# Moving the SBUF addresses of the operands of an expert layer so that each stationary block starts 64 bytes after its moving rows, modulo 512

## The chip, the cores and the metric

The kernel runs on one core of one Trainium2 chip. The metric is the time of one execution in microseconds of device time. The numbers given as "before" come from three executions that were only timed, and from one further execution that the hardware profiler recorded; that one is the source of all rows below.

## The reference

The input x holds 32 sequences of 512 tokens with 256 channels, in float32. What is computed, cut to what matters here:

```python
x  = L0_attn_x                              # 32 x 512 x 256
xn = layernorm(x)
x  = x + attention(xn, Wq, Wk, Wv, Wo, ...) + experts(xn, gate_w, w1, w2)

# attention: 16 heads of 16 channels, no softmax: scores are multiplied by a decay mask
scores = einsum('bhid,bhjd->bhij', q, k) * mask
out    = einsum('bhij,bhjd->bhid', scores, v)   # then Wo and a group norm

# experts: 8 of them; each takes the 128 tokens of a sequence with the highest probability
probs        = softmax(einsum('BTC,CE->BTE', x, gate_w), axis=-1)
top_p, top_i = top_k(probs.transpose(0, 2, 1), 128)
xin = take(x, top_i)                            # 32 x 8 x 128 x 256
h   = gelu(einsum('BElC,ECH->BElH', xin, w1))   # w1: 8 x 256 x 1024
y   = einsum('BElH,EHC->BElC', h, w2)           # w2: 8 x 1024 x 256
out = zeros.at[top_i].add(y * top_p)
```

## The kernel before

The work is written by hand, one instruction stream for each engine, with semaphores between them; no scheduler decides an order. There are two parts, one after the other.

**Attention** runs over the 32 sequences b, in a software pipeline: while sequence b has its scores and values computed, b+1 has its queries, keys and values projected and b-1 its output projection. Products in which accuracy matters are split: every float32 operand is held as a high part (`x_hi`, `w_hi`) and a low part (`x_lo`, `w_lo`) of type float32r, and a product is the sum of three matmuls, high by high, high by low, low by high. The projections of queries, keys and outputs (`query_key`, `project`, through `product`, L1383) have the weights as stationary operand and 512 token columns as moving operand. The projection of values and gate scores (`value_gate`, L1449, L1451, L1453) has 128 tokens as stationary operand and 272 or 256 weight columns as moving operand.

**The experts** follow in 64 steps. A step n is one expert e and a group of four sequences (512 chosen tokens, `SL`; one half of them is `HALF`, 256). The order is `ORDER`: experts 0 and 1 alternate in blocks of four groups, then experts 2 to 7 come one after the other with eight steps each. In a step, TensorE does:

- eight transposes of the gathered rows (`transposes`, L1688), which are moving 128 columns of an identity;
- the first expert matrix as seven products of quadrants (a Strassen-Winograd scheme, `product1` to `product7`, all through `quarter`, L1698): seven products, two halves A and B of each, two column blocks, three terms, which is 84 matmuls. Stationary is a block of 128 columns of `w1h` or `w1l`, moving are the 256 columns of one slot of `xs_hi` or `xs_lo`;
- the second expert matrix (`down`, L1779): four token blocks, eight pieces of the hidden dimension, three terms, which is 96 matmuls. Stationary is a block of 128 tokens of `g_hi` or `g_lo` (the hidden values after the gelu, split), moving are the 256 columns of one piece of `w2h` or `w2l`.

That is 188 matmuls a step, each with a weight load of its own. The weights of an expert are split on ScalarE (high parts) and GpSimd (low parts) while the expert before runs; they have two sets of buffers, index `e % 2`, so that even experts read one set of addresses and odd experts the other. `xs_hi`, `xs_lo`, `g_hi` and `g_lo` have one set.

The expert part has no memory of its own: nearly all its tiles lie over tiles of the attention part, at addresses that are written out as numbers (`at(name, shape, dtype, offset)`), while the attention's tiles get theirs one behind the other (`sb`). A column block of a stationary operand and a slot, piece or token row of a moving operand begin a multiple of 512 bytes after their tile, so the tile's start modulo 512 holds for all of them. The starts modulo 512 before, and the distance d = (stationary start minus moving start) modulo 512 that follows:

```
product                     stationary      moving          d
w1, even experts            w1h, w1l   0    xs_hi/lo 160    352 (high and low weights)
w1, odd experts, high       w1h      128    xs_hi/lo 160    480
w1, odd experts, low        w1l      160    xs_hi    160    0
w2, even experts            g_hi/lo  160    w2h, w2l 128    32
w2, odd experts, w2h        g_hi/lo  160    w2h      160    0
w2, odd experts, w2l        g_hi     160    w2l 160 or 64   0 or 96 (pieces 0-3 or 4-7)
attention, L1383            w, 448          x, a      96    352
attention, L1449-L1453      x, 96           vg, w    448/0  160 or 96
```

The instruction stream interleaves the weight load for the next matmul with the matmul that is running, so the moving rows of one matmul and the stationary block of the next are read at the same time. Inside a step the next block stands at the same distance as the own one, with few exceptions at the seams between products.

Of the kernel before, what the change touches and what calls it, by code (L numbers as in the profile page):

```python
# [42 lines left out]
NSUB = S // SUB  # L43
# [4 lines left out]
GRP = 4  # L48
# [192 lines left out]
def layer(nc, x, xn_d, out, wq, wk, wv, wo, gw, w1, w2, bvr, cst_d, vec_d):  # L241
    with ExitStack() as ctx:
        def sb(name, shape, dt=F32):
            return ctx.enter_context(nc.sbuf_tensor(name, shape, dt))

        def at(name, shape, dt, offset):

            return nc.alloc_sbuf_tensor_at(name, shape, dt, offset=offset)

        def sem(name):  # L250
            return ctx.enter_context(nc.semaphore(name))

# [13 lines left out]
        w_lo = [sb(f"w_lo{i}", [P, DH, D], F32R) for i in range(4)]
        vg_hi = sb("vg_hi", [P, DH, VG], F32R)
        xb = [sb(f"x{i}", [P, TT, D]) for i in range(2)]
        xn = sb("xn", [P, TT, D])
        vraw = sb("v_unbiased", [P, TT, VG])  # L270
        st = sb("ln_stats", [P, TT, 6])
        mv = sb("ln_mv", [P, TT, 2])
        ln_ve, ln_r, ln_y, ln_a, ln_m = (sb(f"ln_{n}", [P, TT]) for n in ("ve", "r", "y", "a", "m"))
        x_hi = sb("x_hi", [P, DH, S], F32R)
        x_lo = sb("x_lo", [P, DH, S], F32R)
        q32 = sb("q32", [P, DH, S])
        qm = [sb(f"q_parity{i}", [P, DH, 2, S]) for i in range(2)]
        qd = [sb(f"q_decayed{i}", [P, DH, S]) for i in range(2)]
        k32 = [sb(f"k{i}", [P, DH, S]) for i in range(2)]
        kn = sb("k_natural", [P, TT, D])  # L280
        vm = [sb(f"v_parity{i}", [P, TT, VW]) for i in range(2)]
        tm = [sb(f"state{i}", [P, NSUB - 1, DH, 2 * HD]) for i in range(2)]
        s_sb = [sb(f"s_sb{i}", [P, PAIRS, 512]) for i in range(2)]
        a_hi = sb("a_hi", [P, DH, S], F32R)
        a_lo = sb("a_lo", [P, DH, S], F32R)
        o32 = sb("o32", [P, DH, S])
        ost = sb("o_stats", [P, DH, 6])
        gm = sb("g_moments", [P, DH, 2])
        gs = sb("g_means", [P, DH, 2])
        gn_ve, gn_r, gn_y, gn_a, gn_m, gn_s, gn_b = (sb(f"gn_{n}", [P, DH])  # L290
                                                     for n in ("ve", "r", "y", "a", "m", "s", "b"))
# [19 lines left out]
        ln_mv = sem("ln_mv_ready")  # L311
# [65 lines left out]
        def has(b):  # L377
# [2 lines left out]

        SL = GRP * CAP
        HALF = SL // 2
        K1 = 7 * QF * 4
        K2 = FT * D * 4
        KX = 7 * HALF * 4
        LATE = 186880
        w1h = [at("w1_hi0", [P, 7, QF], F32R, LATE), at("w1_hi1", [P, 7, QF], F32R, 56448)]
        w1l = [at("w1_lo0", [P, 7, QF], F32R, LATE + K1), at("w1_lo1", [P, 7, QF], F32R, 167584)]
        s2 = at("w2_stage", [P, FT, D], F32, LATE + 2 * K1)
# [3 lines left out]
        xg = [at(f"xg{k}", [P, D], F32, 53248 + 1024 * k if k < 3 else LATE + 2 * K1 + K2) for k in range(GRP)]  # L393
        idx = at("step_idx", [P, GRP], U32, LATE + 2 * K1 + K2 + 1024)
        sidx = at("scatter_idx", [P, GRP], U32, LATE + 2 * K1 + K2 + 1056)
        xs_hi = at("xs_hi", [P, 7, HALF], F32R, 87712)
        xs_lo = at("xs_lo", [P, 7, HALF], F32R, 87712 + KX)
        xsum = at("x_sums", [P, 4, HALF], F32, 87712 + 2 * KX)
        hid = {q: at(f"hidden{q}", [P, 2, 2, HALF], F32, o)
               for q, o in (("22", 114336), ("21", 118432), ("11", 122528), ("12", 130720))}  # L400
        y = [at("y", [P, GRP, D], F32, 126624), res]
# [1509 lines left out]
```

## Time and profile before

| what | value |
|---|---|
| median of three timed runs | 2347.25 us (2346.27 to 2350.14) |
| profiled execution, its time | 2340.57 us |
| profiled execution, its span (first to last instruction) | 2338.6 us |
| matmuls, and weight loads | 34252 each |
| TensorE (PE) busy | 2264.5 us, 97% of the span |
| VectorE, ScalarE, GpSimd busy | 1531.5, 1391.5, 1283.3 us (65, 59, 55%) |

The profile lists what each engine did and when. PE is TensorE's matmuls and PEld its weight loads, which run beside them. Matmuls are pipelined: a row of one matmul is longer than the time until the next one starts, so the pace of a stream of matmuls is read from the distance between starts, or from the length of a window and the count in it, not from a row's duration. The span ends with the expert part, which begins at about 895 us.

### The profile page before, as it was taken

How to read it: one execution, taken by the hardware profiler on the slowest of the kernel's cores; microseconds unless marked ns; L12 is line 12 of the kernel's file. 1: busy time of each engine (PE TensorE's matmuls, PEld its weight loads, DVE VectorE, ACT ScalarE, POOL GpSimd, SP SyncE). 2: the span in 40 equal slices, each digit the busy share in tenths (PEclk: the TensorE clock that was granted, in tenths of full speed). 3: DMA queues.
4: the chain of work that ended last, by engine and by line, in shares of the span. 5: the costliest groups of instructions: out<-in, count | busy, mean ns of one | idle time of the engine just before them, and what ended most of it. 6: DMA issues, size and time to landing. Idle time of an engine off the chain costs nothing.

```text
span 2338.6 us, 81411 instructions
## 1 busy us (share of the span) xinstructions
PE 2264.5 (97%) x34252; PEld 2095.6 (90%) x34252; DVE 1531.5 (65%) x3103; ACT 1391.5 (59%) x2553; POOL 1283.3 (55%) x2012
## 2 busy tenths in 40 slices
PE   6999999999999988999999999999999999999998
PEld 5777777777777778999999999999999999999998
DVE  3555555656666657996766767667667667676674
ACT  4555565555655546556666656666666666666664
POOL 4444444444544455655566666666566576575453
PEclk9999999999999999999999999999999999999999
DMA  3232222322223312232324324224234233232332
GB/s 120 74 95 85 75 76 83 94 84 76 76 75 94 98 61 71 49 77 50 50 44 89 46 46 91 43 49 86 47 52 82 47 54 80 48 54 43 51 50 33
DMA packets 129368, 157.72 MB, mean 67 GB/s; under 512 B 11008, under 2 KB 118656, under 8 KB 129024
## 3 DMA queue, kind: packets, MB, share of 16 engines
q0 software_dynamic: 49152, 67.14, 17.8%
q1 hardware_dynamic: 79872, 85.54, 11.6%
q8 instruction: 272, 4.46, 0.8%
q14 instruction: 72, 0.59, 0.1%
HBM read 85.53 MB, written 67.11 MB: 65 GB/s over the span
## 4 chain that ended last, share of the span: by engine, by line
PE 55%; DVE 0%; POOL 0%; issue 0%; ACT 0%; DVEq 0%
PE attn L1779 28%; PE scores L1698 18%; PE front L1698 7%; PE front L1688 2%; POOL out L798 0%; DVE rows L211 0%; DVE topi L207 0%; DVE top L202 0%; DVE hidden L1263 0%; DVE xs_lo L1233 0%; ACT res L949 0%; DVE rows L223 0%; PE scores L233 0%; PE scores L232 0%; DVE rows L225 0%
## 5 line engine op out<-in xcount | busy, mean ns | idle before, releaser
L1779 PE MATMUL attn<-w_hi,g_hi 128*128 128x256 f32 x2048 | 581.5, 284 | 2.5 <-DVE g_lo L1274 2.4
L1779 PE MATMUL attn<-w_lo,g_hi 128*128 128x256 f32 x2048 | 578.3, 282 | 0.0
L1779 PE MATMUL attn<-w_hi,g_lo 128*128 128x256 f32 x2048 | 578.1, 282 | 0.0
L987 ACT ACTIVATE hidden<-hidden 128x512 f32<-128x512 f32 x384 | 235.4, 629 | 263.9 <-DVE hidden L1263 263.9
L1779 PEld LDWEIGHTS attn<-w_hi,g_hi 128*128 128x128 f32 x2048 | 388.6, 190 | 3.0 <-DVE g_lo L1274 2.7
L1779 PEld LDWEIGHTS attn<-w_hi,g_lo 128*128 128x128 f32 x2048 | 388.3, 190 | 0.0
L1779 PEld LDWEIGHTS attn<-w_lo,g_hi 128*128 128x128 f32 x2048 | 388.0, 189 | 0.0
L1698 PE MATMUL scores<-xs_hi,w_hi 128*128 128x256 f32 x1280 | 362.0, 283 | 8.4 <-DVE xs_lo L1233 6.3
L1698 PE MATMUL scores<-xs_lo,w_hi 128*128 128x256 f32 x1280 | 362.8, 283 | 0.0
L1263 DVE TENSOR_TENSOR hidden<-front,hidden 128x512 f32<-128x512 f32 x256 | 176.3, 689 | 284.0 <-PE front L1698 270.7
L1698 PE MATMUL scores<-xs_hi,w_lo 128*128 128x256 f32 x1280 | 361.0, 282 | 0.0
L1274 DVE TENSOR_TENSOR g_lo<-hidden,g_hi 128x512 fp32r<-128x512 f32 x512 | 348.3, 695 | 9.9 <-ACT g_hi L991 7.6
L718 POOL DMA_INDIRECT out<-y,scatter_idx x128 | 220.3, 1721 | 235.6 <-ACT y L949 206.1
L708 POOL DMA_INDIRECT xg<-xn_rows,step_idx x256 | 278.0, 1086 | 101.3 <-issue 64.2
L718 POOL DMA_INDIRECT out<-res,scatter_idx x124 | 212.6, 1714 | 203.6 <-ACT res L949 167.5
L1698 PEld LDWEIGHTS scores<-xs_hi,w_hi 128*128 128x128 f32 x1280 | 243.3, 190 | 9.9 <-issue 9.2
L1698 PEld LDWEIGHTS scores<-xs_lo,w_hi 128*128 128x128 f32 x1280 | 243.0, 190 | 0.0
L1698 PEld LDWEIGHTS scores<-xs_hi,w_lo 128*128 128x128 f32 x1280 | 242.8, 190 | 0.0
L1263 DVE TENSOR_TENSOR hidden<-scores,hidden 128x512 f32<-128x512 f32 x256 | 172.5, 691 | 78.3 <-PE scores L1698 77.0
L1123 DVE TENSOR_TENSOR s_sb<-scores,cst 128x1024 f32<-128x1024 f32 x128 | 149.8, 1212 | 83.4 <-PE scores L1490 83.4
L610 POOL TENSOR_TENSOR v_parity<-v_unbiased,bv_rows 128x256 f32<-128x256 f32 x128 | 92.2, 730 | 152.2 <-ACT v_unbiased L848 149.7
L991 ACT ACTIVATE g_hi<-hidden 128x512 fp32r<-128x512 f32 x256 | 161.8, 632 | 6.1
(182 smaller groups left out, 5154.4 us busy)
## 6 DMA issues: line engine op xcount, KB each, us to landing
x<-in_x SPq DMA_DIRECT2D x32, 512.0 KB, 5.3
w_stage<-in_w SPq DMA_DIRECT2D x16, 1024.0 KB, 6.4
xn_rows<-xn SPq DMA_DIRECT2D x32, 512.0 KB, 3.2
res<-in_x SPq DMA_DIRECT2D x32, 512.0 KB, 3.8
out<-res SPq DMA_DIRECT2D x32, 512.0 KB, 3.4
xg<-xn_rows,step_idx POOLq DMA_INDIRECT x256
out<-y,scatter_idx POOLq DMA_INDIRECT x128, 3.9
out<-res,scatter_idx POOLq DMA_INDIRECT x128, 3.9
```

Source lines behind the costliest of these rows:

```text
L610: pool.tensor_tensor(own, spread(vraw[:, t, 0:D]), spread(bv[:]), ALU.add).then_inc(vm_ready, 1)
L708: pool.indirect_dma_start(xg[k][:], None, xn_d, bass.IndirectOffsetOnAxis(idx[:, k:k + 1], 0)).then_inc(gathered, 16)
L718: pool.indirect_dma_start(out_rows, bass.IndirectOffsetOnAxis(sidx[:, k:k + 1], 0), y[g % 2][:, k, :], None, compute_op=ALU.add).then_inc( ...
L987: act.activation(own(q, p), src, ACT.Gelu).then_inc(g_ready, 1)
L991: act.activation(quadrant(g_hi, q, p), own(q, p), ACT.Copy).then_inc(gh_act, 1)
L1123: dve.tensor_tensor(s_sb[z][:, banks, :].rearrange("p k (g i) -> p (k g) i", i=SUB), sbk[:, banks, :].rearrange("p k (g i) -> p (k g) i", ...
L1263: dve.tensor_tensor(dst, a, b, ALU.add).then_inc(sum_ready, 1)
L1274: dve.tensor_tensor(quadrant(g_lo, q, p), own(q, p), quadrant(g_hi, q, p).bitcast(F32), ALU.subtract).then_inc(gl_ready, 1)
L1688: last = pe.transpose(tb[:, h, k * P:(k + 1) * P], xg[k][:, h * P:(h + 1) * P], ident)
L1698: last = pe.matmul(dst, w_[par][:, w, cols], x__[:, x_, :], start=first and m == 0 and i == 0, stop=i == 2, skip_group_check=True)
L1779: last = pe.matmul(yb[k % 2][:, 0:D], g_[:, m, cols], w, start=start and m == first and i == 0, stop=end, skip_group_check=True)
```

## The change

Only SBUF addresses change. Every instruction of every engine is the same in number, order, shape and semaphores as before; the order of the program shows no other difference than the names of buffers. Small tiles move to the front of the memory, the attention's large tiles get written-out addresses at multiples of 512 (`tm[1]` and the first column block of `vraw` aside), and the expert part's tiles are laid out anew over them. The starts modulo 512 after:

```
product                     stationary      moving          d
w1, all experts             w1h, w1l   0    xs_hi/lo 448    64
w2, all experts             g_hi/lo   64    w2h, w2l   0    64
attention, L1383            w          0    x, a       0    0
attention, L1449-L1453      x          0    vg, w   0/64    0 or 448
```

The core of the diff:

```diff
-        w_hi = [None if i == 2 else sb(f"w_hi{i}", [P, DH, D], F32R) for i in range(4)]
-        x_hi = sb("x_hi", [P, DH, S], F32R)
-        x_lo = sb("x_lo", [P, DH, S], F32R)
...
+        KB = 1024
+        w_hi = [None if i == 2 else at(f"w_hi{i}", [P, DH, D], F32R, o * KB)
+                for i, o in enumerate((54, 56, None, 58))]
...
+        x_hi = at("x_hi", [P, DH, S], F32R, 143 * KB)
+        x_lo = at("x_lo", [P, DH, S], F32R, 147 * KB)
...
-        LATE = 186880
-        w1h = [at("w1_hi0", [P, 7, QF], F32R, LATE), at("w1_hi1", [P, 7, QF], F32R, 56448)]
-        w1l = [at("w1_lo0", [P, 7, QF], F32R, LATE + K1), at("w1_lo1", [P, 7, QF], F32R, 167584)]
-        w2h = [at("w2_hi0", [P, FT, D], F32R, 78976), at("w2_hi1", [P, FT, D], F32R, 106144)]
-               for i, os in enumerate(((70784, 74880), (181920, LATE + 2 * K1 + K2 + 1088)))]
-        xs_hi = at("xs_hi", [P, 7, HALF], F32R, 87712)
-        xs_lo = at("xs_lo", [P, 7, HALF], F32R, 87712 + KX)
-        g_hi = at("g_hi", [P, FT, SL], F32R, 134816)
-        g_lo = at("g_lo", [P, FT, SL], F32R, 151200)
...
+        G_AT = 87 * KB + 64
+        X_AT = 143 * KB + 448
+        w1h = [at("w1_hi0", [P, 7, QF], F32R, 183 * KB + 512), at("w1_hi1", [P, 7, QF], F32R, 57 * KB)]
+        w1l = [at("w1_lo0", [P, 7, QF], F32R, 197 * KB + 512), at("w1_lo1", [P, 7, QF], F32R, 169 * KB + 512)]
+        w2h = [at("w2_hi0", [P, FT, D], F32R, 79 * KB), at("w2_hi1", [P, FT, D], F32R, 157 * KB + 512)]
+               for i, os in enumerate(((71 * KB, 75 * KB), (165 * KB + 512, 219 * KB + 512)))]
+        g_hi = at("g_hi", [P, FT, SL], F32R, G_AT)
+        g_lo = at("g_lo", [P, FT, SL], F32R, G_AT + FT * SL * 4)
+        xs_hi = at("xs_hi", [P, 7, HALF], F32R, X_AT)
+        xs_lo = at("xs_lo", [P, 7, HALF], F32R, X_AT + 7 * HALF * 4)
```

## Rows read from the trace of the kernel before

**Rows 1.** The page's part 1 (busy us, share, count) and TensorE's granted clock.

```profile
PE 2264.5 (97%) x34252; PEld 2095.6 (90%) x34252; DVE 1531.5 (65%) x3103; ACT 1391.5 (59%) x2553; POOL 1283.3 (55%) x2012
...
PEclk9999999999999999999999999999999999999999
```

**Rows 2.** Windows: experts 2 to 5, eight steps each (length, busy us and count, clock).

```profile
1271.44:1448.63 177.19, 177.19 (x1506) 177.19 (x1505) 122.27 (x225) 112.78 (x208) 113.56 (x100) 1.00 0.33 60
1448.63:1626.96 178.33, 178.33 (x1506) 178.33 (x1505) 122.43 (x225) 112.76 (x208) 114.06 (x100) 1.00 0.33 60
1626.96:1804.16 177.19, 177.19 (x1506) 177.19 (x1505) 122.27 (x225) 112.79 (x208) 113.53 (x100) 1.00 0.33 61
1804.16:1982.49 178.33, 178.33 (x1506) 178.33 (x1505) 122.75 (x225) 112.89 (x208) 113.76 (x100) 1.00 0.33 60
```

**Rows 3.** Groups by form: TensorE's matmuls (count, busy us, mean ns, idle before).

```profile
L1779 PE MATMUL attn<-w_hi,g_hi 128*128 128x256 f32 x2048 | 581.5, 284 | 2.5 <-DVE g_lo L1274 2.4
...
L1698 PE MATMUL scores<-xs_hi,w_hi 128*128 128x256 f32 x1280 | 362.0, 283 | 8.4 <-DVE xs_lo L1233 6.3 <-DVE res L1170 1.7 <-DVE hidden L1263 0.5
...
L1698 PE MATMUL front<-xs_hi,w_hi 128*128 128x256 f32 x512 | 144.2, 282 | 0.0
...
L1383 PE MATMUL front<-x_hi,w_hi 128*128 128x512 f32 x256 | 109.0, 426 | 4.0 <-DVE x_lo L1136 4.0
...
L1449 PE MATMUL front<-vg_hi,x_hi 128*128 128x272 f32 x256 | 86.9, 339 | 0.0
...
L1383 PE MATMUL front<-a_hi,w_hi 128*128 128x512 f32 x124 | 49.7, 401 | 0.0
```

**Rows 4.** Timeline of TensorE, expert 4: transposes (start us, duration us, instruction).

```profile
1651.23 1.04 PE L1688 MATMUL front<-cst,xg 128*128 128x128 f32 x8
1652.03 0.37 PE L1779 MATMUL attn<-w_hi,g_hi 128*128 128x256 f32 x1
1652.23 0.28 PE L1779 MATMUL attn<-w_lo,g_hi 128*128 128x256 f32 x1
```

**Rows 5.** Timeline, expert 4, w2 pieces: first and last of 24 matmuls, d = 32.

```profile
1654.24 0.28 PE L1779 MATMUL attn<-w_hi,g_hi 128*128 128x256 f32 x1
...
1656.96 0.28 PE L1779 MATMUL attn<-w_hi,g_lo 128*128 128x256 f32 x1
```

**Rows 6.** Timeline, expert 5, w2 pieces 0-3: first and last of 24, d = 0.

```profile
1831.60 0.28 PE L1779 MATMUL attn<-w_hi,g_hi 128*128 128x256 f32 x1
...
1834.36 0.28 PE L1779 MATMUL attn<-w_hi,g_lo 128*128 128x256 f32 x1
```

**Rows 7.** Timeline, expert 4, w1 products: first and last of 36 matmuls, d = 352.

```profile
1666.99 0.28 PE L1698 MATMUL scores<-xs_hi,w_hi 128*128 128x256 f32 x1
...
1671.15 0.28 PE L1698 MATMUL front<-xs_hi,w_lo 128*128 128x256 f32 x1
```

**Rows 8.** Timeline, expert 1, one w1 product: two neighbouring column blocks, d = 0.

```profile
1201.89 0.28 PE L1698 MATMUL front<-xs_lo,w_hi 128*128 128x256 f32 x1
1202.00 0.28 PE L1698 MATMUL front<-xs_hi,w_lo 128*128 128x256 f32 x1
...
1202.24 0.29 PE L1698 MATMUL front<-xs_lo,w_hi 128*128 128x256 f32 x1
1202.37 0.28 PE L1698 MATMUL front<-xs_hi,w_lo 128*128 128x256 f32 x1
```

**Rows 9.** Timeline, attention, 512 moving columns: first and last of six matmuls, d = 352.

```profile
599.78 0.40 PE L1383 MATMUL front<-a_hi,w_hi 128*128 128x512 f32 x1
...
600.95 0.39 PE L1383 MATMUL front<-a_hi,w_lo 128*128 128x512 f32 x1
```

**Rows 10.** Timeline of weight loads beside Rows 9: two neighbours.

```profile
600.25 0.19 PEld L1383 LDWEIGHTS front<-a_hi,w_hi 128*128 128x128 f32 x1
600.49 0.19 PEld L1383 LDWEIGHTS front<-a_lo,w_hi 128*128 128x128 f32 x1
```

**Rows 11.** Window: attention, 300 to 800 us (columns as in Rows 2).

```profile
300.00:800.00 500.00, 483.99 (x12925) 386.50 (x12924) 306.42 (x737) 284.25 (x527) 233.56 (x729) 1.00 0.28 85
```

**Rows 12.** The page's part 4: the chain that ended last.

```profile
PE attn L1779 28%; PE scores L1698 18%; PE front L1698 7%; PE front L1688 2%; POOL out L798 0%; DVE rows L211 0%; DVE topi L207 0%; DVE top L202 0%; DVE hidden L1263 0%; DVE xs_lo L1233 0%; ACT res L949 0%; DVE rows L223 0%; PE scores L233 0%; PE scores L232 0%; DVE rows L225 0%
```

More of the change, by code:

```diff
@@ L254, in layer @@
         vec = sb("vec", [P, V_N])
+        gst_w = sb("gate_stage", [P, DH, E])
+        st = sb("ln_stats", [P, TT, 6])
+        mv = sb("ln_mv", [P, TT, 2])
+        ln_ve, ln_r, ln_y, ln_a, ln_m = (sb(f"ln_{n}", [P, TT]) for n in ("ve", "r", "y", "a", "m"))
+        ost = sb("o_stats", [P, DH, 6])
+        gm = sb("g_moments", [P, DH, 2])
+        gs = sb("g_means", [P, DH, 2])
+        gn_ve, gn_r, gn_y, gn_a, gn_m, gn_s, gn_b = (sb(f"gn_{n}", [P, DH])
+                                                     for n in ("ve", "r", "y", "a", "m", "s", "b"))
+        idx = sb("step_idx", [P, GRP], U32)
+        sidx = sb("scatter_idx", [P, GRP], U32)
         route = Routing(ctx, nc, cst)
@@ L261, in layer @@
         wst = s1[:, 0:4, :].rearrange("p a (b n) -> p (a b) n", n=D).rearrange("p (i h) n -> p i h n", h=DH)
-        gst_w = sb("gate_stage", [P, DH, E])
-        bv = sb("bv_rows", [P, D])
-        w_hi = [None if i == 2 else sb(f"w_hi{i}", [P, DH, D], F32R) for i in range(4)]
[L266 to L270, printed above, removed]
@@ L271, in layer @@
-        st = sb("ln_stats", [P, TT, 6])
-        mv = sb("ln_mv", [P, TT, 2])
-        ln_ve, ln_r, ln_y, ln_a, ln_m = (sb(f"ln_{n}", [P, TT]) for n in ("ve", "r", "y", "a", "m"))
-        x_hi = sb("x_hi", [P, DH, S], F32R)
-        x_lo = sb("x_lo", [P, DH, S], F32R)
[L276 to L289, printed above, removed]
@@ L290, in layer @@
-        gn_ve, gn_r, gn_y, gn_a, gn_m, gn_s, gn_b = (sb(f"gn_{n}", [P, DH])
-                                                     for n in ("ve", "r", "y", "a", "m", "s", "b"))
+        KB = 1024
+        bv = at("bv_rows", [P, D], F32, 53 * KB)
+        w_hi = [None if i == 2 else at(f"w_hi{i}", [P, DH, D], F32R, o * KB)
+                for i, o in enumerate((54, 56, None, 58))]
+        w_lo = [at(f"w_lo{i}", [P, DH, D], F32R, (60 + 2 * i) * KB) for i in range(4)]
+        xb = [at(f"x{i}", [P, TT, D], F32, (68 + 4 * i) * KB) for i in range(2)]
@@ new lines, in layer @@
+        xn = at("xn", [P, TT, D], F32, 76 * KB)
+        vg_hi = at("vg_hi", [P, DH, VG], F32R, 80 * KB)
+        vraw = at("v_unbiased", [P, TT, VG], F32, 80 * KB + DH * VG * 4)
+        tm = [at(f"state{i}", [P, NSUB - 1, DH, 2 * HD], F32, 90 * KB - (2 - i) * (NSUB - 1) * DH * 2 * HD * 4)
+              for i in range(2)]
+        kn = at("k_natural", [P, TT, D], F32, 90 * KB)
+        k32 = [at(f"k{i}", [P, DH, S], F32, o * KB) for i, o in enumerate((127, 94))]
+        qd = [at(f"q_decayed{i}", [P, DH, S], F32, o * KB) for i, o in enumerate((131, 98))]
@@ new lines, in layer @@
+        qm = [at(f"q_parity{i}", [P, DH, 2, S], F32, o * KB) for i, o in enumerate((135, 102))]
+        vm = [at(f"v_parity{i}", [P, TT, VW], F32, 110 * KB + i * TT * VW * 4) for i in range(2)]
+        x_hi = at("x_hi", [P, DH, S], F32R, 143 * KB)
+        x_lo = at("x_lo", [P, DH, S], F32R, 147 * KB)
+        q32 = at("q32", [P, DH, S], F32, 151 * KB)
+        s_sb = [at(f"s_sb{i}", [P, PAIRS, 512], F32, (155 + 8 * i) * KB) for i in range(2)]
+        a_hi = at("a_hi", [P, DH, S], F32R, 171 * KB)
@@ L293, in layer @@
+        a_lo = at("a_lo", [P, DH, S], F32R, 175 * KB)
+        o32 = at("o32", [P, DH, S], F32, 179 * KB)
         tb = ctx.enter_context(nc.psum_tensor("front", [P, DH, 512], F32))
@@ new lines, in layer @@
+        w2h = [at("w2_hi0", [P, FT, D], F32R, 79 * KB), at("w2_hi1", [P, FT, D], F32R, 157 * KB + 512)]
+        w2l = [[at(f"w2_lo{i}{j}", [P, FT // 2, D], F32R, o) for j, o in enumerate(os)]
+               for i, os in enumerate(((71 * KB, 75 * KB), (165 * KB + 512, 219 * KB + 512)))]
+        xg = [at(f"xg{k}", [P, D], F32, (53 + k) * KB) for k in range(GRP)]
+        g_hi = at("g_hi", [P, FT, SL], F32R, G_AT)
+        g_lo = at("g_lo", [P, FT, SL], F32R, G_AT + FT * SL * 4)
+        hid = {q: at(f"hidden{q}", [P, 2, 2, HALF], F32, G_AT + o * KB)
+               for q, o in (("22", 32), ("21", 36), ("11", 44), ("12", 48))}
```

14 lines of the change are left out of this document (3 added, 11 removed).

## The prediction

> **What bounds the kernel now.** I read the page first. TensorE's matmuls are busy for 97% of the span, no other engine for more than 65% [rows 1]. The granted clock stands at its upper level (2.4 GHz) in all 40 slices, so the clock has nothing to give. The chain that ended last is TensorE almost alone: `down` 28%, the w1 products 25%, the transposes 2%; every entry of another engine rounds to nothing [rows 12].
>
> Next come windows cut at the borders of single experts [rows 2]. In each of them TensorE's busy time is the window's whole length, while VectorE has 122 of 177 us, ScalarE and GpSimd 113. So from there to the end no wait is on the path, and a nanosecond more or less for each matmul goes into the time undiminished. The windows also show how regular this is: the two even experts take 177.19 us, the two odd ones 178.33, to the last digit, with the same instructions. All that differs is the buffer set, that is, the addresses. Eight steps of 188 matmuls make 1504 (two more records reach over the edges), so a step is 22.149 us in an even expert and 22.291 in an odd one. The eight transposes and the first matmul after them take 1652.23 − 1651.23 = 1.00 us [rows 4]; the other 179 matmuls take (22.149 − 1.00) / 179 = 118.15 ns each in even experts and 118.94 in odd ones. The counts of the whole program, three terms of each row, are 3 × 2048 in `down` and 3 × (1280 + 512) in the w1 products [rows 3], 11520 in all, 180 for each of the 64 steps.
>
> One column per clock would be 256 / 2.4 = 106.7 ns. So each of these matmuls takes about 11.8 ns longer than its columns alone. That is the sum the change could draw on; the question is how much of it comes from two reads of SBUF that meet, the running matmul's moving rows and the next one's stationary block.
>
> **What the trace says on the distance d.** The timeline gives paces at three distances. 24 matmuls at d = 32 take (1656.96 − 1654.24) / 23 = 118.3 ns each [rows 5], 24 at d = 0 take 120.0 [rows 6], 36 at d = 352 take 118.9 [rows 7]. Addresses matter more at single places: in one w1 product of an odd expert, where d = 0 for the low weights, the matmul with `xs_lo` takes 0.11 us in one column block and 0.13 in the next [rows 8]; 512 bytes are all that separates the two blocks. The distance 64 occurs nowhere.
>
> How much can the meeting of the reads cost at all? In attention six matmuls with 512 moving columns and d = 352 start 234.0 ns apart [rows 9]. A weight load begins with each and its record is 0.19 us long [rows 10]; the eight loads of the transposes pass in 0.80 us [rows 4], so a load reads for at most about 100 ns. The second half of a 512-column matmul thus has no load beside it. With 118.9 ns for the first half (the same d, a load beside it) the second takes 234.0 − 118.9 = 115.1. So most of the extra 11.8 ns is there without any load, and a load at d = 352 adds about 3.8.
>
> **The change part by part.** It removes and adds no instruction, DMA or wait; nothing moves in a queue. The terms are three.
>
> First, all 11456 matmuls of the expert part that count here (179 × 64) go to d = 64. From below their pace is bounded by the matmul without a load, 115.1 ns; from above by the slowest long stretch, 120.0. The nearest rows are those at d = 32. I take 117.2, about a third of the way from 118.3 down to the floor: one distance everywhere does away with the dear places (d = 0, in most of the odd experts' matmuls), and a block that keeps a fixed lead over the rows should meet them less often, but rows 32 bytes beside it show no deep dip, so I do not take more. Even experts then gain 118.15 − 117.2 = 0.95 ns, odd ones 118.94 − 117.2 = 1.74; half of the steps each, 1.345 × 11456 = 15.4 us less. At the floor it would be 3.445 × 11456 = 39.5 us less, at 120.0 it would be 1.455 × 11456 = 16.7 us more.
>
> Second, attention's split products leave d = 352 (and 160 or 96) for d = 0 (or 448). They are 3 × (256 + 124) with 512 columns and 3 × 256 in `value_gate` [rows 3], 1908. At worst each pays the difference between d = 0 and d = 32, 120.0 − 118.3 = 1.7 ns, 3.2 us; at best nothing. TensorE is busy for 484 of 500 us there [rows 11], so nearly all of it would reach the path; I take 3 us.
>
> Third, the other engines' tiles move too. Where they work slower, 55 us in 177 on VectorE hide it in the expert part [rows 2]; I take nothing. If that cover were gone, TensorE would wait at L1698 for `xs_lo`, where it idles for 6.3 us now [rows 3].
>
> The sum is −15.4 + 3 = −12.4 us. The profiled execution took 2340.57 us, 6.7 below the median of the timed ones; I apply the difference to the median: 2347.25 − 12.4 = 2335.
>
> **A rule against it.** The product with two paces [rows 8] and the 177.19 against 178.33 us [rows 2] say that TensorE's reads do get in each other's way, by 1 to 10 ns. The Trainium skill says otherwise: "TensorE: Matmul & The Clock Gate" (Part 2, step 1) gives the weight load and the moving operand an independent SBUF read port each, and "SBUF — State Buffer" (Who interferes with whom) states "PE and ACT never wait on anyone". By that rule the sum would be zero and the time 2347; the trace does not agree with it.
>
> **The rivals.** *Distance does nothing* (0.25). The reads' cost may hang on higher address bits or on the phase that the stream happens to be in; 512 bytes turned 0.11 into 0.13 us without a change of d [rows 8], which speaks for it. Then 64 is like 32: a pace of 118.3 in both kinds of expert changes +0.15 and −0.64 ns, on the mean −0.245 × 11456 = −2.8 us, and attention's 3 us give it back: 2347, between 2342 and 2352.
>
> *Blocks on equal phase are the slow ones* (0.23), the rival on the other side. d = 0 and d = 64 share that block and rows start at the same place within 64 bytes; d = 32, 96, 352 and 480 do not. The 120.0 of [rows 6] would then be the price of that equality, and all expert matmuls would pay it: +16.7 + 3.2 = +19.9 us, 2367. Against it: half the blocks of [rows 8] take 0.11 us at d = 0. It decides once the common pace is above the present mean of 118.55; with attention's loss, from 118.3 on the kernel is no faster.
>
> *The whole extra time goes* (0.06). If the moving rows wait only because of how loads lie, the pace falls to 106.7 ns: 11.85 × 11456 = 136 us, 2211. The second halves at 115.1 without a load speak against it [rows 9, 10].
>
> **How the numbers follow.** The forecast case, a pace between 115.1 and 118, has 0.46; its own range is 2308 to 2342. A measurement of this kernel can tell 0.2%, some 4.7 us, from no change. Faster are the forecast case, the last rival and a few hundredths at the edge of the first: 0.54. The rest of the first makes "same" 0.23 after a little of it goes either way; slower has 0.23. The range from 2308 (the floor, attention unchanged) to 2360 leaves out the last rival and the dear end of the second, under 2 in 10.
>
> **What would show it.** In the windows of single experts, even and odd ones should have one length, near 8 × (1.00 + 179 × 0.1172) = 175.8 us. If they stay at 177 to 178 the first rival holds; at 179.8 (120.0 ns) the second; at 160.8 the third. The two column blocks of [rows 8] should take the same time. The 512-column matmuls of [rows 9] should stand at 234 to 236 ns. I am wrong if a distance that the trace has never shown behaves unlike its neighbours, which is where my 117.2 is chosen and not read; or if VectorE's or ScalarE's groups get longer and TensorE shows idle time in the expert windows.

## The result, and the profile after

The changed kernel takes 2316.52 us (median of four runs, 2313.94 to 2321.24); the kernel before takes 2346.76 beside it (four runs, 2346.1 to 2350.14). The ratio is 0.9871, with a 95% interval from 0.9852 to 0.9889: faster by 30.2 us, where 12.4 were forecast. The profiled execution is the slowest of the four, 2321.24 us, with a span of 2319.3.

On the page of the kernel after, TensorE's busy time (part 1) and its granted clock (part 2) answer to [rows 1]. TensorE is busy for 29.6 us less, in the same number of matmuls:

```profile
PE 2234.9 (96%) x34252; PEld 2068.1 (89%) x34252; DVE 1522.3 (66%) x3103; ACT 1390.6 (60%) x2553; POOL 1271.4 (55%) x2012
...
PEclk9999999999999998999999999999999999999999
```

Windows of experts 2 to 5 of the kernel after, with the columns of [rows 2] (behind the clock stand the busy share of the DMA engines and GB/s):

```profile
1271.90:1446.33 174.43, 174.43 (x1506) 174.43 (x1505) 121.48 (x225) 112.61 (x208) 112.00 (x100) 1.00 0.34 60
1446.33:1620.75 174.43, 174.43 (x1506) 174.43 (x1505) 121.46 (x225) 112.51 (x208) 112.60 (x100) 1.00 0.34 61
1620.75:1795.18 174.43, 174.43 (x1506) 174.43 (x1505) 121.50 (x225) 112.60 (x208) 111.98 (x100) 1.00 0.34 62
1795.18:1969.61 174.43, 174.43 (x1506) 174.43 (x1505) 121.47 (x225) 112.57 (x208) 112.36 (x100) 1.00 0.34 62
```

Even and odd experts now have one length, TensorE still fills the whole window, and the other engines are as busy as before. An even expert is 2.76 us shorter and an odd one 3.90 [rows 2]; carried over to all eight experts, four of each make 11.0 + 15.6 = 26.6 us, nearly all of the gain. A step is 174.43 / 8 = 21.80 us and the mean pace (21.80 − 1.00) / 179 = 116.2 ns.

That mean hides two paces. The timeline of TensorE in expert 4 of the kernel after shows first and last of 24 `down` matmuls, then the first, the fourth and the last of 36 w1 matmuls:

```profile
1713.05 0.28 PE L1779 MATMUL attn<-w_hi,g_hi 128*128 128x256 f32 x1
...
1715.75 0.28 PE L1779 MATMUL attn<-w_hi,g_lo 128*128 128x256 f32 x1
...
1725.66 0.29 PE L1698 MATMUL scores<-xs_hi,w_hi 128*128 128x256 f32 x1
...
1726.02 0.28 PE L1698 MATMUL scores<-xs_hi,w_hi 128*128 128x256 f32 x1
...
1729.65 0.28 PE L1698 MATMUL front<-xs_hi,w_lo 128*128 128x256 f32 x1
```

`down` runs at (1715.75 − 1713.05) / 23 = 117.4 ns to the digits shown (117.7 with the trace's nanoseconds), as forecast. The w1 stretch starts with 0.12 us a matmul and from the fourth on takes (1729.65 − 1726.02) / 32 = 113.4 ns, 113.33 by the nanoseconds: 272 clocks at 2.4 GHz for 256 columns, the same from matmul to matmul. That is below the 115.1 that the prediction took for a floor. Both stand at d = 64. The alternation of [rows 8] is gone.

In attention, six matmuls with 512 columns answer to [rows 9], d now 0 (timeline, kernel after):

```profile
601.92 0.39 PE L1383 MATMUL front<-a_hi,w_hi 128*128 128x512 f32 x1
...
603.05 0.39 PE L1383 MATMUL front<-a_hi,w_lo 128*128 128x512 f32 x1
```

They start (603.05 − 601.92) / 5 = 226 ns apart instead of 234.0; over all output projections of the trace the mean is 226.7 (544 clocks). The query and key projections, twice as many, come down less: they start 229.8 ns apart on the mean, 233.9 before, because each run of them opens with about five starts of 228 to 236 ns before it settles at 226.7.

One thing the profiled execution lost has another cause. Its first `down` begins at 911.1 us, 12.5 later than before (898.6). Up to the last but one group norm of attention (848.1 us, 846.8 before) the lag is 1.3 us; the rest arises at the passage from attention to the experts. A window of it, first before and then after:

```profile
855.00:905.00 50.00, 39.53 (x824) 35.17 (x824) 32.44 (x75) 25.66 (x45) 23.46 (x48) 0.90 0.29 87
865.00:915.00 50.00, 36.05 (x663) 31.72 (x653) 31.60 (x68) 17.27 (x28) 13.51 (x33) 0.75 0.24 76
```

The granted clock there is 0.75 on the mean, 0.90 before: for half of the 50 us it is at the lower of its two levels (1.2 and 2.4 GHz), where before it was for a fifth. TensorE is busy for 36 of them. Two runs of one and the same program, below as e2 and e11, reach the first `down` at 912.5 and 897.3 us. So some 15 us between single executions need not come from addresses, and below I read causes from windows and paces and take a single time only as a rough check.

### The profile page after: what moved, and what is told of

Read it like the earlier page. It is cut to its first block, busy times and chain, and to the rows that moved or that the text cites. A ratio compares the mean times of both kernels' runs of the same rounds, so it can differ in the third digit from the quotient of the medians.

```text
span 2319.3 us, 81411 instructions
## 1 busy us (share of the span) xinstructions
PE 2234.9 (96%) x34252; PEld 2068.1 (89%) x34252; DVE 1522.3 (66%) x3103; ACT 1390.6 (60%) x2553; POOL 1271.4 (55%) x2012
## 3 DMA queue, kind: packets, MB, share of 16 engines
q1 hardware_dynamic: 79872, 85.54, 11.5%
## 4 chain that ended last, share of the span: by engine, by line
PE 54%; DVE 0%; POOL 0%; issue 0%; ACT 0%; DVEq 0%
PE attn L1779 28%; PE scores L1698 17%; PE front L1698 7%; PE front L1688 2%; POOL out L798 0%; DVE rows L211 0%; DVE topi L207 0%; DVE top L202 0%; DVE hidden L1263 0%; DVE xs_lo L1233 0%; ACT res L949 0%; DVE rows L223 0%; PE scores L233 0%; PE scores L232 0%; DVE rows L225 0%
## 5 line engine op out<-in xcount | busy, mean ns | idle before, releaser
L1698 PE MATMUL scores<-xs_lo,w_hi 128*128 128x256 f32 x1280 | 356.4, 278 | 0.0
L1698 PE MATMUL scores<-xs_hi,w_lo 128*128 128x256 f32 x1280 | 356.0, 278 | 0.0
L1274 DVE TENSOR_TENSOR g_lo<-hidden,g_hi 128x512 fp32r<-128x512 f32 x512 | 340.7, 685 | 9.5 <-ACT g_hi L991 7.0
L718 POOL DMA_INDIRECT out<-y,scatter_idx x128 | 214.7, 1677 | 222.1 <-ACT y L949 192.6
```

The lines of the kernel that those rows point to most:

```text
L718: pool.indirect_dma_start(out_rows, bass.IndirectOffsetOnAxis(sidx[:, k:k + 1], 0), y[g % 2][:, k, :], None, compute_op=ALU.add).then_inc( ...
L1274: dve.tensor_tensor(quadrant(g_lo, q, p), own(q, p), quadrant(g_hi, q, p).bitcast(F32), ALU.subtract).then_inc(gl_ready, 1)
L1698: last = pe.matmul(dst, w_[par][:, w, cols], x__[:, x_, :], start=first and m == 0 and i == 0, stop=i == 2, skip_group_check=True)
```

## The experiments

All of them change addresses only, against the kernel after; the expected texts were written in three batches (e1 to e4, e5 to e8, e9 to e12), each on one chip with runs of the kernel before, and each names its theories anew. A pair below is (stationary start, moving start) modulo 512. A seam is the place where one product follows another; its distance is that of the new product's first block to the rows of the old product's last matmul. "Step" is the mean of eight steps, even experts / odd experts; before it is 22.15 / 22.29 us, after 21.80 / 21.80.

| run | w1 pair, even / odd | w2 pair, even / odd | step | time, us | before, same chip |
|---|---|---|---|---|---|
| e1 | 0,448 / 0,448 | 0,0 / 0,448 | 21.93 / 21.29 | 2312.68 | 2347.40 |
| e2 | 0,160 / 0,160 | 32,0 / 32,0 | 22.17 / 22.17 | 2346.07 | 2347.40 |
| e3 | 0,0 / 0,0 | 0,0 / 0,256 | 22.46 / 22.46 | 2354.47 | 2347.40 |
| e4 | 0,448 / 0,448 | 64,0 / 64,0 | 21.80 / 21.80 | 2327.01 | 2347.40 |
| e5 | 0,448 / 0,448 | 0,448 / 0,448 | 21.29 / 21.29 | 2281.48 | 2341.94 |
| e6 | 32,480 / 0,480 | 128,0 / 128,0 | 22.09 / 22.16 | 2334.42 | 2341.94 |
| e7 | 0,384 / 0,384 | 256,0 / 256,0 | 22.30 / 22.30 | 2341.76 | 2341.94 |
| e8 | 64,0 / 0,0 | 448,0 / 448,0 | 21.63 / 22.17 | 2312.41 | 2341.94 |
| e9 | 64,0 / 0,0 | 64,0 / 64,0 | 21.78 / 22.07 | 2319.69 | 2341.13 |
| e10 | 64,0 / 0,0 | 0,448 / 0,0 | 21.94 / 22.33 | 2331.24 | 2341.13 |
| e11 | as e2 | as e2 | 22.17 / 22.17 | 2335.95 | 2341.13 |
| e12 | 0,64 / 0,64 | 0,0 / 0,64 | 22.31 / 22.08 | 2336.80 | 2341.13 |

(In odd experts of e6, e8, e9 and e10 the low weights of w2's pieces 4 to 7, a sixth of `down`, start at 32, 64, 64 and 448 instead. Times are single ones, but for the medians of e5, five runs, and e11, seven; of before there are one, nine and ten runs in the three batches.)

**e1: hidden values at 0, second matrix of odd experts at 448.**

```diff
-        G_AT = 87 * KB + 64
+        G_AT = 87 * KB
-        ... at("w2_hi1", [P, FT, D], F32R, 157 * KB + 512)
+        ... at("w2_hi1", [P, FT, D], F32R, 157 * KB + 448)
-        ... (165 * KB + 512, 219 * KB + 512)
+        ... (165 * KB + 448, 219 * KB + 960)
```

> g_hi and g_lo start at 0 modulo 512 instead of 64; in odd experts w2 moves to 448, in even experts it stays at 0. So w2 has d = 0 in even experts and d = 64 in odd ones; w1 stays at d = 64 (stationary 0, moving 448). In the changed kernel the 24 w2 matmuls of pieces 0-3 go at 117.7 ns in both kinds of expert, the 36 w1 matmuls at 113.9. Theory 1 (the distance modulo 512 sets the pace): w2 of odd experts stays at 117.7, w2 of even experts goes up towards 120, so a step takes 21.80 us in odd and about 22.0 us in even experts. Theory 2 (the stationary block's own start decides, a multiple of 512 is fast): w2 goes to about 113.5 in both, a step takes about 21.4 us in both. Theory 3 (the moving rows' start decides, a multiple of 64 is fast): no change, 117.7 and 21.80 us in both.

Windows of expert 4 and expert 5, columns as above:

```profile
1618.05:1793.49 175.44, 175.44 (x1506) 175.44 (x1505) 121.57 (x225) 113.22 (x208) 112.06 (x100) 1.00 0.34 62
1793.49:1963.81 170.32, 170.32 (x1506) 170.32 (x1505) 122.45 (x225) 112.38 (x208) 113.82 (x100) 1.00 0.34 62
```

Even experts, with `down` at d = 0, have it at 120.00 ns (24 matmuls from 1710.88 to 1713.64 us). Odd ones, with `down` at d = 64, at 113.35 (1883.62 to 1886.23), with the w1 products at 113.34 too. The direction is that of the distance, but the same d = 64 in `down` is 117.7 in the kernel after and 113.35 here: d is not all.

**e2: back to distances that the kernel before had (w2 d = 32, w1 d = 352), at new places.**

```diff
-        G_AT = 87 * KB + 64
-        X_AT = 143 * KB + 448
+        G_AT = 87 * KB + 32
+        X_AT = 143 * KB + 160
```

> g at 32 and xs at 160 modulo 512: the distances of the even experts of the kernel before, d = 32 for w2 and d = 352 for w1, now in all experts, everything else as in the changed kernel. Theory 1 (distance modulo 512): the paces of before come back, w2 about 118.3, w1 about 118.9, a step of 22.15 us. Theory 2 (stationary start): w1 stays at 113.9 since its stationary blocks stay at 0, w2 about 118. Theory 3 (moving start): w1 goes to about 118, since its rows now start 32 bytes beside a multiple of 64, w2 stays at 117.7. Rival 4 (higher address bits, that is, the new places as such): both stay near 113.9 and 117.7.

```profile
1633.92:1811.30 177.38, 177.38 (x1506) 177.38 (x1505) 122.28 (x225) 112.84 (x208) 113.64 (x100) 1.00 0.33 61
1811.30:1988.69 177.39, 177.39 (x1506) 177.39 (x1505) 122.28 (x225) 112.84 (x208) 114.11 (x100) 1.00 0.34 61
```

In the windows of experts 4 and 5 the length of the even experts before [rows 2] is back, to 0.2 us, and for odd experts as well. The paces are 118.4 in `down` and 118.7 in w1, those of [rows 5, 7] within 0.2 ns. The layout itself is therefore worth nothing in the expert part: the start modulo 512 is what counts, not higher address bits and not which tile lies where.

**e3: everything at distance 0 or 256.**

```diff
-        G_AT = 87 * KB + 64
-        X_AT = 143 * KB + 448
+        G_AT = 87 * KB
+        X_AT = 143 * KB
-        ... "w2_hi1", ... 157 * KB + 512    ... (165 * KB + 512, 219 * KB + 512)
+        ... "w2_hi1", ... 157 * KB + 256    ... (165 * KB + 256, 219 * KB + 768)
```

> g and xs at 0 modulo 512, so w1 has d = 0 with both operands at 0; w2 has d = 0 in even experts, and in odd experts its rows are at 256, so d = 256. Theory 1 (distance): d = 0 is slow, w1 and the w2 of even experts at about 119 to 120. Theory 2 (stationary start): everything at about 113.5, a step of 21.3 to 21.4 us in both kinds of expert. Theory 3 (moving start): no change from the changed kernel, 113.9 and 117.7.

```profile
1633.38:1813.06 179.68, 179.68 (x1507) 179.68 (x1505) 122.78 (x225) 112.55 (x208) 114.16 (x100) 1.00 0.33 60
1813.06:1992.74 179.68, 179.68 (x1507) 179.68 (x1505) 122.89 (x225) 112.66 (x208) 114.17 (x100) 1.00 0.33 60
```

Both experts' windows are 179.68 us, and w1 as well as `down` stand at 120.00 ns, 288 clocks, at d = 0 and at d = 256. Stationary blocks that start at a multiple of 512 are in e3 as in e1 and e5, so that alignment by itself gains nothing.

**e4: attention's weights back to d = 352.**

```diff
-        bv = at("bv_rows", [P, D], F32, 53 * KB)
+        bv = at("bv_rows", [P, D], F32, 53 * KB - 160)
...          (w_hi and w_lo: each offset - 160)
```

> Only attention: its weights (w_hi, w_lo) and the bias rows start 160 bytes lower, so that the projections with 512 moving columns have d = 352 again, as in the kernel before, with the moving rows still at a multiple of 64. Six such matmuls start 234.0 ns apart in the kernel before, about 226.5 in the changed one (d = 0). Theory 1 (distance) and theory 2 (stationary start): about 234 again. Theory 3 (the moving rows' start): stays at 226.5. The expert steps stay at 21.80 us under all of them.

Six matmuls with 512 columns, as above:

```profile
607.17 0.39 PE L1383 MATMUL front<-a_hi,w_hi 128*128 128x512 f32 x1
...
608.34 0.39 PE L1383 MATMUL front<-a_hi,w_lo 128*128 128x512 f32 x1
```

They stand at (608.34 − 607.17) / 5 = 234 ns again. The moving rows lie where they lie in the kernel after, so it is not the rows' own alignment. The block's own start moved together with the distance, so this run alone does not tell these two apart. A sequence takes 26.92 us here and 26.65, 26.70 and 26.59 in e1, e2 and e3 on the same chip (twenty sequences, from the group norm's matmul L1574 of sequence 6 to that of sequence 26), about 0.27 less with d = 0. That is an indication only: e5 to e8, with the attention of the kernel after, spread from 26.10 to 26.50 on one chip.

**e5: one pair, 0 and 448, in every expert product, so that the seams between products are at d = 64 too.**

```diff
-        G_AT = 87 * KB + 64
+        G_AT = 87 * KB
-        ... at("w1_hi1", [P, 7, QF], F32R, 57 * KB)
+        ... at("w1_hi1", [P, 7, QF], F32R, 56 * KB + 512)
-        w2h = [... 79 * KB), ... 157 * KB + 512)]
+        w2h = [... 79 * KB - 64), ... 157 * KB + 448)]
-        ... ((71 * KB, 75 * KB), (165 * KB + 512, 219 * KB + 512))
+        ... ((71 * KB - 64, 75 * KB - 64), (165 * KB + 448, 219 * KB + 960))
...          (xg and one small softmax tile give way)
```

> Both expert matrices in all experts on the pair that ran at 113.33 ns, stationary blocks at 0 and moving rows at 448 modulo 512 (g at 0; w1 weights at 0; xs and all of w2 at 448). Theory 1 (the pair of starts sets the pace, whatever the product): all 179 matmuls of a step at about 113.3 ns, a step of 21.29 us in even and odd experts, 33 us less than the changed kernel's 64 steps of 21.80: a time of about 2284 us, ratio to the kernel before near 0.973. Rival (the odd experts' tiles owe their pace to their places in memory, not to the start modulo 512): even experts stay near 21.9 us, the time near 2312.

The median of five runs is 2281.48 us (2280.09 to 2285.46), the ratio to the kernel before 0.9745, from 0.9722 to 0.9769. It beats both kernels. Windows of experts 4 and 5:

```profile
1598.83:1769.13 170.30, 170.30 (x1507) 170.30 (x1505) 122.47 (x225) 112.18 (x208) 113.46 (x100) 1.00 0.34 63
1769.13:1939.42 170.29, 170.29 (x1506) 170.29 (x1505) 122.43 (x225) 112.08 (x208) 113.69 (x100) 1.00 0.34 63
```

A step of 21.29 us is a mean of (21.29 − 1.00) / 179 = 113.3 ns: every matmul is at 272 clocks. Against before, 32 × (22.15 − 21.29) + 32 × (22.29 − 21.29) = 59.5 us, where 60.5 are measured. Yet the timeline of the same execution shows 24 `down` matmuls at 117.8 ns, (1036.36 − 1033.65) / 23, in step 5, a stop behind them, and later 24 at 113.0, (1691.55 − 1688.95) / 23 (113.35 by the nanoseconds):

```profile
1033.65 0.28 PE L1780 MATMUL attn<-w_hi,g_hi 128*128 128x256 f32 x1
...
1036.36 0.28 PE L1780 MATMUL attn<-w_hi,g_lo 128*128 128x256 f32 x1
1039.33 0.36 PE L1699 MATMUL scores<-xs_hi,w_hi 128*128 128x256 f32 x1 [2.69 <-DVE xs_lo L1234]
...
1688.95 0.28 PE L1780 MATMUL attn<-w_hi,g_hi 128*128 128x256 f32 x1
...
1691.55 0.28 PE L1780 MATMUL attn<-w_hi,g_lo 128*128 128x256 f32 x1
```

The pair is the same and the code is the same. So d = 64 allows two paces. Once it goes on after that stop, and the clock is back at its upper level, the stream is at 113.3, and from step 7 on, where TensorE no longer stops, it keeps that pace to the end.

**e6: distances 64 in even, 32 in odd w1; 128 in `down`.**

```diff
-        G_AT = 87 * KB + 64
-        X_AT = 143 * KB + 448
+        G_AT = 87 * KB + 128
+        X_AT = 143 * KB + 480
...          (w1_hi0, w1_lo0, w2_stage and the last w2_lo tile: each + 32)
```

> Looks at other pairs. w1 has the rows at 480: in even experts the weights start at 32 (d = 64, both starts 32 beside a multiple of 64), in odd ones at 0 (d = 32). w2 has g at 128 and rows at 0, d = 128. Theory 1 (d = 64 is fast when the stationary block does not run over a multiple of 512): even w1 near 117.7 like the pair 64 and 0, odd w1 unknown, between 113.3 and 118.4; w2 between 117.7 and 120. Theory 2 (d = 64 is fast when the rows start just below a multiple of 512): even w1 at about 113.5, odd w1 near 118.4 as at d = 32 elsewhere.

```profile
1623.89:1800.58 176.69, 176.69 (x1507) 176.69 (x1505) 122.03 (x225) 112.97 (x208) 113.08 (x100) 1.00 0.33 61
1800.58:1977.86 177.28, 177.28 (x1506) 177.28 (x1505) 122.58 (x225) 112.64 (x208) 113.45 (x100) 1.00 0.33 60
```

The long stretches run at 117.7 (64), 118.3 (32) and 118.9 ns (128). At d = 64 that is not all: in the same steps of the even expert three of the four shorter w1 stretches settle at 113.3. So the pair 32 and 480 has the two paces as well, and the window is shorter than the odd one by only 0.6 us since the longest stretch is at the dearer one. In the odd expert no w1 stretch comes below 117.7.

**e7: distances 128 in w1, 256 in `down`.**

```diff
-        G_AT = 87 * KB + 64
-        X_AT = 143 * KB + 448
+        G_AT = 87 * KB + 256
+        X_AT = 143 * KB + 384
```

> w1: weights at 0, rows at 384, d = 128. w2: g at 256, rows at 0, d = 256. Theory 1 (a stationary block that does not run over a multiple of 512 is fast at any small lead): w1 at about 113.5. Theory 2 (64 alone is fast): w1 at 117 to 120. For w2 both expect 120, as the pair 0 and 256 had.

```profile
1625.57:1803.97 178.40, 178.40 (x1506) 178.40 (x1505) 122.44 (x225) 112.96 (x208) 113.63 (x100) 1.00 0.33 60
```

The pace is 118.7 ns for 128 and 120.00 for 256. A distance of 256 is as dear as a distance of 0.

**e8: w1 of even experts as 64 and 0 instead of 0 and 448; `down` at 448.**

```diff
-        G_AT = 87 * KB + 64
-        X_AT = 143 * KB + 448
+        G_AT = 87 * KB + 448
+        X_AT = 143 * KB + 512
...          (w1_hi0, w1_lo0, w2_stage and the last w2_lo tile: each + 64)
```

> w1 gets in even experts the very pair that w2 has in the changed kernel, weights at 64 and rows at 0 (d = 64), and in odd experts 0 and 0. w2: g at 448, rows at 0, d = 448. Theory 1 (the pair decides): w1 at 117.7 in even experts and 120.0 in odd ones. Theory 2 (the distance decides and w2 is slower for a reason of its own): w1 at 113.4 to 113.9 in even experts, 120.0 in odd ones. w2 at d = 448 is new: 117 to 120 expected by both.

```profile
1608.85:1781.92 173.07, 173.07 (x1506) 173.07 (x1505) 121.92 (x225) 112.70 (x208) 111.81 (x100) 1.00 0.34 62
1781.92:1959.27 177.35, 177.35 (x1506) 177.35 (x1505) 122.83 (x225) 112.46 (x208) 114.68 (x100) 1.00 0.33 61
```

The two windows, experts 4 and 5, differ in w1, d = 64 against d = 0, which is again 120.00 ns on the mean (and in a sixth of `down`, see under the table). In the even expert the 36 w1 matmuls run at 113.34 ns but a shorter stretch of twelve earlier in the same step at 117.73: the two paces once more, now with 64 and 0. `down`, at d = 448, has them too. Behind the transposes it takes 117.8 ns, but later in the same step 24 `down` matmuls, first and last here, take (1712.58 − 1709.97) / 23 = 113.5 ns (113.35 by the nanoseconds):

```profile
1709.97 0.28 PE L1779 MATMUL attn<-w_hi,g_hi 128*128 128x256 f32 x1
...
1712.58 0.28 PE L1779 MATMUL attn<-w_hi,g_lo 128*128 128x256 f32 x1
```

So a block that starts 64 bytes behind its rows can have the fast pace as well as one that starts 64 bytes ahead.

**e9: the pair 64 and 0 everywhere in even experts, seams too.**

```diff
-        X_AT = 143 * KB + 448
+        X_AT = 143 * KB + 512
...          (w1_hi0, w1_lo0, w2_stage and the last w2_lo tile: each + 64)
```

> In even experts everything is at d = 64 with the other starts: weights of w1 and g at 64, xs and w2 at 0. So d is 64 also at the seams, where a w1 matmul's rows meet the first g block and the other way round. In odd experts the weights of w1 stay at 0, so w1 has d = 0 there, w2 d = 64. Theory 1 (one distance of 64 everywhere, seams too, holds TensorE in its fast pattern of 113.33 ns): even experts take 21.29 us a step as in the kernel with all at 0 and 448. Theory 2 (rows at 448, or blocks at 0, are what is fast): w2 of even experts at 117.7 as in the changed kernel, a step of about 21.8 us. Odd experts: w1 at 120.0 under both.

If a single distance without dear seams were enough, even experts would take 21.29 us a step as in e5. They do not. Windows of the first and the second step of expert 4:

```profile
1615.20:1637.21 22.01, 22.01 (x191) 22.01 (x190) 15.31 (x29) 13.59 (x25) 11.42 (x11) 1.00 0.37 68
1637.21:1658.58 21.37, 21.37 (x190) 21.37 (x189) 15.26 (x29) 14.01 (x27) 14.16 (x13) 1.00 0.31 49
```

Steps alternate, 22.00 and 21.38 us, through the whole expert: in the first all matmuls after the transposes stand at 117.8 ns, in the second all at 113.3. Instructions and addresses are alike from step to step, and TensorE waits in neither. The pace changes at the transposes, where the stream of 256-column matmuls is broken, and holds until the next ones. That expectation fell. What it leaves is that the pace goes with the running stream and not with the addresses alone.

**e10: w1 at 64 and 0, `down` at 0 and 448, to see which of the pairs is fast.**

```diff
-        G_AT = 87 * KB + 64
-        X_AT = 143 * KB + 448
+        G_AT = 87 * KB
+        X_AT = 143 * KB + 512
...          (w1 of even experts + 64; w2h and w2l of even experts - 64, as in e5)
```

> Only the seams: in even experts both products have d = 64, but by different pairs, w1 with weights at 64 and rows at 0, w2 with g at 0 and rows at 448. From w2 to w1 the distance is then 128, from w1 to w2 it is 0; in the changed kernel it is 0 and 128, the other way round. Theory 1 (d = 64 has two lasting paces, and the seam by which a product is entered picks one): w1 now at 117.7 and w2 at 113.33 after a few slow matmuls, the reverse of the changed kernel. Theory 2 (no memory of the seam): both at 113.33, a step of 21.29 us. Theory 3 (the pair 64 and 0 is slow in itself): w1 at 117.7 everywhere, w2 at 113.33. The first w1 stretch after a seam tells theory 1 from 3 only together with the kernel in which 64 and 0 stand everywhere.

Even experts, timeline of one step: 24 `down` matmuls soon behind the transposes, then the fourth and the last of 24 `down` matmuls behind a w1 product:

```profile
1713.16 0.28 PE L1780 MATMUL attn<-w_hi,g_hi 128*128 128x256 f32 x1
...
1715.87 0.28 PE L1780 MATMUL attn<-w_hi,g_lo 128*128 128x256 f32 x1
...
1723.35 0.28 PE L1780 MATMUL attn<-w_hi,g_hi 128*128 128x256 f32 x1
...
1725.62 0.28 PE L1780 MATMUL attn<-w_hi,g_lo 128*128 128x256 f32 x1
```

The first take (1715.87 − 1713.16) / 23 = 117.8 ns, with the pair that runs at 113.3 in all steady steps of e5, so this pair is not the fast one in itself. The second take (1725.62 − 1723.35) / 20 = 113.5 ns (113.3 by the nanoseconds). In the steady steps every `down` stretch behind a w1 product settles at 113.3, and every w1 stretch stands at 117.7 or 117.8: the reverse of the kernel after, as theory 1 expected. Only the stretch behind the transposes does not follow it.

**e11: the kernel of e2, timed, as the part that attention has.**

> The changed kernel with the expert part at the distances of the even experts before (32 and 352), timed: what the attention part's new places are worth alone. Its expert step is 22.17 us against 22.15 and 22.31 before, so that 64 steps give 3.6 us back and all the rest of a difference is attention's and the passage between the parts. If attention gains from d = 0 as its pace says (0.2 us for each of 32 sequences): 2337 against 2347. If it does not: 2343.

2335.95 us (2330.36 to 2345.34, seven runs), ratio 0.9981, from 0.9961 to 1.0. The expert steps at 22.17 account for 32 × (22.15 − 22.17) + 32 × (22.29 − 22.17) = 3.2 of the 5.2 us less; 2 us are left for attention, within the interval's 9 us. By the interval, from no difference to 9.1 us less, attention gained up to 5.9 us or lost up to 3.2; the middle is a small gain, and a loss of 3 lies at the very edge.

**e12: the block 64 bytes behind the rows instead of ahead (odd experts), d = 448.**

```diff
-        G_AT = 87 * KB + 64
-        X_AT = 143 * KB + 448
+        G_AT = 87 * KB
+        X_AT = 143 * KB + 64
-        ... "w2_hi1", ... 157 * KB + 512    ... (165 * KB + 512, 219 * KB + 512)
+        ... "w2_hi1", ... 157 * KB + 64     ... (165 * KB + 64, 219 * KB + 576)
```

> The mirror image: in odd experts blocks at 0 and rows at 64 in both products and at the seams, d = 448 everywhere, so that the stationary block starts 64 bytes behind the rows. In even experts w2 has d = 0. Theory 1 (two reads 64 bytes apart are enough, whichever leads): 113.33 ns, a step of 21.29 us in odd experts. Theory 2 (the block must lead): 117.8 ns as w2 had at 448 and 0, a step of about 22.1 us.

```profile
1623.92:1802.41 178.49, 178.49 (x1506) 178.49 (x1505) 122.56 (x225) 112.89 (x208) 113.46 (x100) 1.00 0.33 61
1802.41:1979.05 176.64, 176.64 (x1507) 176.64 (x1505) 122.35 (x225) 112.62 (x208) 113.93 (x100) 1.00 0.33 60
```

The odd expert, with one pair and seams at d = 448 everywhere, takes 176.64 us, all matmuls at 117.8 and none at 113.3. That is what theory 2 expected, but it does not show that the block must lead. Earlier in the same execution, behind a start that came late (0.17 us between starts), 17 w1 matmuls with this pair (first and last here, the granted clock at its upper level) take (1017.94 − 1016.13) / 16 = 113.1 ns, 113.3 by the nanoseconds:

```profile
1016.13 0.28 PE L1698 MATMUL scores<-xs_lo,w_hi 128*128 128x256 f32 x1
...
1017.94 0.28 PE L1698 MATMUL front<-xs_hi,w_lo 128*128 128x256 f32 x1
```

With the 24 `down` matmuls of e8 it follows that 448 has the two paces of 64.

## Why the prediction was right on the mechanism, and where its size was off

**What bounds the kernel: right.** TensorE fills the expert windows in every run here, VectorE keeps some 50 us of cover in each, and the pace went into the time undiminished (59.5 us by the windows of e5, 60.5 measured). The third term, nothing from the other engines, holds: their busy times in the windows of the kernel after are those of [rows 2] to within about 1 us on VectorE and ScalarE and 2 us on GpSimd.

**That distance modulo 512 decides: right, and shown.** e2 restores the old paces by restoring the old distances; e1, e3 and e8 put 120.00 ns on the long stretches wherever d is 0; e4 brings back attention's pace with attention's distance, though the block's own start would explain that run as well. The rival *distance does nothing* is refuted by these. That the modulus is 512 and not 256 is not shown: 0 and 256 cost the same, and no other two distances that differ by 256 were compared. The rival *blocks on equal phase are the slow ones* has its price right (120.00, for d = 0, and for 256 as well), but d = 64 does not belong to it. The whole of the extra time did not go: 113.33 ns, not 106.7, is the lowest pace in any steady window.

**The size of the first term: the step that failed.** The prediction put the expert part at −15.4 us, at 117.2 ns; the windows give −26.6, at a mean of 116.2. That is only 1 ns less, but 1 ns is 11.5 us here. Of the 17.8 us between −12.4 and −30.2 this term makes 11.2, and the second one, with the passage, the other 6.6. Two things stand in its place. First, the floor of 234.0 − 118.9 = 115.1, taken from the second half of a 512-column matmul that has no load beside it, is wrong by 1.8 ns: at d = 0 the same matmul takes 226.7, twice 113.33, and e1 and e5 hold 113.33 for 256 columns with a load beside each. So, if the first half costs what a 256-column matmul costs (5.4 to 5.6 ns over 113.33 at d = 352), part of the 7.3 ns between 234.0 and 226.7 falls into that second half. Second, "about a third of the way from 118.3 down to the floor" treats 64 as one pace near 32's. It is two paces, 117.75 and 113.33: `down` sits on the first, most of w1 on the second, and the mean lies between. The reason that the prediction gave for its step below 118.3, a block that keeps a fixed lead over its rows, is not borne out either: at 448, where the block is behind, the same two paces occur (e8, e12). That the mean came out near 117.2 owes something to luck, since nothing known then said which of two paces a stretch would take. The range, which went down to the floor at 2308, held the time.

**The second term: wrong sign.** Attention at d = 0 was to cost 3 us. Its 512-column matmuls became faster instead, 7 to 8 ns in the output projections and 4 in those of queries and keys; the prediction had taken the price of d = 0 from 256-column matmuls [rows 6]. By these paces an estimated 372 × 7.7 + 768 × 4.1 ns = 6 us go away. The times show it only roughly: −2 us in e11, with an interval that includes nothing; about 0.27 us a sequence, some 9 us over 32, between e4 and its neighbours, within the spread of single executions. With the experts' −26.6 the 30.2 us measured leave 3.6 for attention and the passage.

**The rule against it: not borne out here.** Addresses alone move the time from 2281 (e5) to 2354 us (e3) with the same instructions. The Trainium skill, "SBUF — State Buffer" (Who interferes with whom), says that TensorE never waits on anyone; whether or not that holds towards other engines, TensorE's pace does depend on how its own blocks and rows lie to each other, by up to 6.67 ns a matmul of 256 columns (120.00 − 113.33). That the two reads meet is the plainest reading of this; no trace shows the reads themselves.

**What stays open.** Which of its two paces a stream at d = 64 or 448 takes. Seen: the same pair at both, within one execution (e5) and from step to step (e9); a change only where the stream is broken, by a stop, the transposes or another pair; then one pace for as long as the stream runs, mostly after two to four matmuls in between. The seam plays a part: in the steady windows every stretch at d = 64 behind a seam at distance 0 took the fast pace (w1 in the kernel after and in the even experts of e1, `down` in e10), and every one behind a seam at 128 the dear one (`down` in the kernel after, w1 in e10). Behind other seams (e6, e8) and behind the transposes (e5, e9) both paces occur. That a relative phase set at the break decides fits all this, but nothing here sets such a phase by itself, so it is not shown. It also is open why d = 0 costs 256-column matmuls 6.67 ns and the settled 512-column ones nothing. All five executions of e5 have its short time (2280 to 2285 us), though only one of them has a trace; no run explains why it gets to the fast pace, and another kernel may not.

## What to carry to other kernels

Where TensorE is the bound and every matmul has a weight load of its own, measure the pace between starts and compare stretches by (stationary start − moving start) modulo 512; in float32r with 256 columns 0 and 256 are the dearest here (120.00 ns), 32, 128 and 352 lie between 118.3 and 118.9, and a block 64 bytes ahead or behind runs at 117.8 or 113.33. Giving every product of the loop one pair, seams included, brought the fast pace throughout with 0 and 448 (e5), every other step with 64 and 0 (e9) and never in the steady steps with 0 and 64 (e12). So try several, and read the steady windows, since a layout can land on either of two paces. And when a floor is worked out by subtracting one row from another, ask what the subtraction assumes: a range that reaches beyond such a floor costs little.

## What the runs showed of the hardware that I had not expected

The lowest steady pace is 113.33 ns for 256 columns and 226.67 for 512: 17 clocks of 2.4 GHz for 16 columns in both. At the lower level of the clock this is gone. In e5 this stretch of thirteen w1 matmuls runs at a granted clock of 0.50 (its window, then first and last start in the timeline):

```profile
1041.20:1043.70 2.50, 2.50 (x13) 2.50 (x13) 1.53 (x3) 0.80 (x2) 1.42 (x1) 0.50 0.00 0
...
1041.15 0.41 PE L1699 MATMUL front<-xs_lo,w_hi 128*128 128x256 f32 x1
...
1043.71 0.41 PE L1699 MATMUL scores<-xs_lo,w_hi 128*128 128x256 f32 x1
```

(1043.71 − 1041.15) / 12 = 213.3 ns, which is 256 / 1.2: one column a clock, nothing more. In e3, at d = 0, a dozen such matmuls at the lower clock (1043.9 to 1046.2 us) start 213 to 214 ns apart too. So the extra sixteenth and the price of the distance were seen only at the upper clock; this is drawn from a few stretches, and no run shows where in TensorE the extra clocks go.
